# A software pipeline of attention and feed-forward: where the layer statistics and the transposed tokens stand in two engines' orders

## What is computed

```python
def _layer(x, wqkv, qs, ksc, wo, lg, lb, w1, b1, w2, b2):   # 8 heads of 64, window 64
    h = shift_token(x)                      # features 64..127 come from the token before
    q, k, v = split(h @ wqkv, 3)
    q = l2norm(q) * qs;  k = l2norm(k) * ksc
    q, k = rotary_xpos(q, k)
    x = x + local_attention(q, k, v) @ wo   # each window of 64 sees itself and the one before
    h = shift_token(x)
    mu = h.mean(-1, keepdims=True);  var = h.var(-1, keepdims=True)
    h = (h - mu) / jnp.sqrt(var + 1e-05) * lg + lb
    a, g = split(h @ w1 + b1, 2)            # 341 columns each
    return x + (a * gelu(g)) @ w2 + b2
```

## Time and profile before

| What | Value |
|---|---|
| median of 3 runs | 2008.37 us (2007.29 to 2013.43) |
| the profiled execution's own time | 2013.04 us |
| its span, first to last instruction | 2011.2 us |
| busy share of the span | PE 83%, DVE 65%, ACT 59%, POOL 54% |
| mean granted TensorE clock | 0.934 of full speed |

### The profile page before, as it was taken

How to read it: one execution, slowest core, us unless ns; L and a number is a source line. 1 busy time by engine, 2 the same in 40 slices (tenths; PEclk the granted TensorE clock), 3 DMA queues, 4 the chain that set the end, 5 groups by cost and what they waited for, 6 DMA issues and landing times. The chain is left out here.

```text
span 2011.2 us, 47115 instructions
## 1 busy us (share of the span) xinstructions
PE 1662.8 (83%) x18545; PEld 1149.5 (57%) x18545; DVE 1314.9 (65%) x2041; ACT 1195.2 (59%) x1972; POOL 1085.8 (54%) x631
## 2 busy tenths in 40 slices
PE   1389997899999348999999649899999899999953
PEld 1356665566666216776767426666666666666642
DVE  3378885555445508999999557777776766667532
ACT  0166666344444115777777428777787777777742
POOL 0166663344444206767677567666666666666403
PEclk9999999999999668999999879999999999999986
DMA  3100000000000020000000101111111111111101
GB/s 100 47 2 2 3 2 9 13 7 7 12 6 0 9 85 2 2 2 2 3 2 2 59 22 28 25 26 23 23 23 23 28 23 23 22 25 23 26 16 42
DMA packets 52352, 40.20 MB, mean 20 GB/s; under 512 B 24424, under 2 KB 44172, under 8 KB 52020
## 3 DMA queue, kind: packets, MB, share of 16 engines
q1 hardware_dynamic: 52148, 37.35, 7.3%
HBM read 15.75 MB, written 2.13 MB: 9 GB/s over the span
## 5 line engine op out<-in xcount | busy, mean ns | idle before, releaser
L438 POOL TENSOR_TENSOR a_prob<-a_prob,a_top 128x1024 f32<-128x1024 f32 x192 | 359.7, 1894 | 133.8 <-DVE a_top L651 133.8
L645 DVE TENSOR_TENSOR a_prob<-ps,a_table 128x1024 f32<-128x1024 f32 x192 | 226.2, 1220 | 112.9 <-PE ps L505 56.6
L612 ACT ACTIVATE a_probT<-ps 128x1024 f32<-128x1024 f32 x192 | 196.4, 1023 | 91.6 <-PE ps L515 91.6
L877 POOL TENSOR_TENSOR e_hh<-e_h,e_hh 128x512 fp32r<-128x512 f32 x112 | 144.2, 1290 | 197.1 <-ACT e_hh L864 195.4
L651 DVE TENSOR_REDUCE a_top<-a_prob 128x4 f32<-128x1024 f32 (+1 forms) x192 | 225.2, 1215 | 9.1 <-issue 0.4
L515 PEld LDWEIGHTS ps<-ident,a_prob 128*128 128x128 f32 x1536 | 168.7, 142 | 95.3 <-issue 61.0
L607 ACT ACTIVATE a_prob<-a_prob 128x1024 f32<-128x1024 f32 x192 | 202.4, 1054 | 32.5 <-POOL a_prob L438 32.5
L515 PE MATMUL ps<-ident,a_prob 128*128 128x128 f32 x1536 | 209.8, 280 | 7.6 <-ACT a_probT L612 2.6
L1115 POOL TENSOR_TENSOR i_qk<-i_raw,i_rot 128x1024 f32<-128x1024 f32 x64 | 151.9, 2374 | 83.6 <-ACT i_raw L1323 83.6
L1167 PE MATMUL ps<-i_wqkv,i_hT 128*128 128x512 f32 x256 | 144.6, 693 | 51.8 <-issue 25.1
L898 DVE TENSOR_TENSOR e_h<-ps,e_sg 128x512 f32<-128x512 f32 x112 | 77.4, 691 | 145.3 <-PE ps L764 124.7
(11 more groups left out here) (198 smaller groups left out, 3687.0 us busy)
## 6 DMA issues: line engine op xcount, KB each, us to landing
i_V<-i_V SPq DMA_DIRECT2D x96, 130.0 KB, 2.3
a_prob<-skew_scratch SPq DMA_DIRECT2D x2, 2048.0 KB, 9.4
X<-in_L_attn_x SPq DMA_DIRECT2D x4, 512.0 KB, 6.0
a_table<-in_c_l_table SPq DMA_DIRECT2D x1, 2048.0 KB, 8.2
e_xs<-Y SPq DMA_DIRECT2D x8, 256.0 KB, 2.3
i_ms<-Y SPq DMA_DIRECT2D x16, 128.0 KB
out_dram<-X SPq DMA_DIRECT2D x4, 512.0 KB, 3.3
i_ms<-Y SPq DMA_DIRECT2D x16, 127.0 KB
```

The costliest lines, as they stand in the source:

```text
L438: nc.gpsimd.tensor_tensor(s, s, top[:, slot].unsqueeze(2).broadcast_to([P, HG, KW]), ALU.subtract).then_inc(shifted, 1)
L612: nc.scalar.activation(probT[:, n % 4].rearrange("p (b n) -> p b n", b=2), ps[:, 4:6, :], ACT.Copy).then_inc(pT_sb, 1)
L645: nc.vector.tensor_tensor(prob[:, slot].rearrange("p (b x) k -> p b x k", b=2), ps[:, 2 * (n % 2):2 * (n % 2) + 2, :].rearrange("p b (x k) ...
```

## The change

Nothing is computed in another way but for one operation, which changes its engine. In each engine's loop over `step`:

- SP: `stage(R)` now comes ahead of `window_values(step + 1)` in its step.
- ScalarE: `inverse_deviation(R)` goes from the end of step 4R+6 into step 4R+7, behind `keep_probT` and ahead of `exp`. `keep_mlp_tokens(R)` is gone from ScalarE.
- VectorE: `deviations(R)` goes from the start of step 4R+7 to its end, behind `quotient`, and `keep_mlp_tokens(R)`, now a multiplication and an addition on VectorE, follows it at once. At the end of a step `keep_value` now stands ahead of `moments`.

```diff
@@ SP
             for step in range(FIRST, LAST):
-                if is_tile(step + 1):
-                    window_values(step + 1)
                 R, c = round_at(step, 5)
                 if R is not None and c == 0:
                     stage(R)
+                if is_tile(step + 1):
+                    window_values(step + 1)
@@ ScalarE
-            def keep_mlp_tokens(R):
-                l = layer(4 * R)
-                act.wait_ge(m_T, R + 1)
-                after(act, ga_ps, R * NC)
-                nc.scalar.activation(mT[:, :], ps[:, 0, :], ACT.Identity, scale=vecs[:, l, 0:1], bias=vecs[:, l, 1:2]).then_inc(m_sb, 1)
-
...
                 if is_tile(step - 1):
                     keep_probT(step - 1)
+                R, c = round_at(step, 7)
+                if R is not None and c == 0:
+                    inverse_deviation(R)
                 if is_tile(step):
                     exp(step)
...
-                R, c = round_at(step, 6)
-                if R is not None and c == 0:
-                    inverse_deviation(R)
-                R, c = round_at(step, 7)
-                if R is not None and c == 0:
-                    keep_mlp_tokens(R)
@@ VectorE
+            def keep_mlp_tokens(R):
+                l = layer(4 * R)
+                dve.wait_ge(m_T, R + 1)
+                after(dve, ga_ps, R * NC)
+                nc.vector.tensor_scalar(mT[:, :], ps[:, 0, :], vecs[:, l, 0:1], vecs[:, l, 1:2], ALU.mult, ALU.add).then_inc(m_sb, 1)
+
...
-                R, c = round_at(step, 7)
-                if R is not None and c == 0:
-                    deviations(R)
                 if is_tile(step + LEAD - 1):
                     square_sums(step + LEAD - 1)
...
                 if is_tile(step - 1):
                     quotient(step - 1)
+                R, c = round_at(step, 7)
+                if R is not None and c == 0:
+                    deviations(R)
+                    keep_mlp_tokens(R)
+                R, c = round_at(step, 8)
+                if R is not None and c < NC:
+                    keep_value(R, c)
                 R, c = round_at(step, 6)
                 if R is not None and c == 0:
                     moments(R)
-                R, c = round_at(step, 8)
-                if R is not None and c < NC:
-                    keep_value(R, c)
                 dve.drain()
```

## The result

| | Before | After |
|---|---|---|
| median | 2009.17 us (2007.29 to 2013.43) | 2023.5 us (2021.86 to 2024.25) |
| ratio, 95% interval | 1 | 1.0061 (1.0041 to 1.0082) |
| the profiled execution | 2013.04 us | 2024.25 us |

The changed kernel is slower by 14 us by the medians (by 12 by the ratio), where +6.8 was forecast: 2023.5 us against 2015. That is inside the range of 1992 to 2025, but above what rival A, the forecast, gave itself (2008 to 2022). To see where the time lies, both profiles are cut at three events: the first mask addition, the L1167 behind round 0's token copy, and the same L1167 twelve rounds later.

The account below looks back on a forecast made before the run. The bound was TensorE's 2.08 us wait for ScalarE's token copy each round, with the low clock behind it. Twelve rounds at +16.2 us and the ends at -9.4 gave +6.8, a median of 2015 us; range 1992 to 2025.

Parts of the forecast that it names:

- rival A: The forecast itself: deviations held beside GpSimd in step 4R+7, 2015 us, its own range 2008 to 2022; chance 0.47.
- Points 1 and 2: VectorE, end of step 4R+6: reduction starts 1.1 us earlier; ScalarE, start of step 4R+7: its work moves up 0.66 us.
- Point 3: VectorE, end of step 4R+7: a small deviation operation is held until GpSimd's L1118 ends, deviations end at 1702.35, not 1700.2.
- Point 4: TensorE's seam into step 4R+8: with the token copy on VectorE (0.75 us), L1167 starts 1.4 us later each round.
- Point 5: TensorE's clock: idle 4.1 us instead of 2.08, low stretch costs 1.4 us a round; twelve rounds make +16.2 us.
- rival D: Deviations held, with a second low-clock stretch in each round: 2.2 us a round for the clock, 2025 us; chance 0.10.
- C: Deviations held, but the low clock falls mostly on idle time: 0.7 us a round, 2007 us, no change; chance 0.18.
- Point 6: Sync queue: V copies' delay behind the stage stays hidden, some 8 us to spare; no wait and no gain in full rounds.
- Point 7: The ends gain: -4 us in round 0, 0 in round 13, -1.7 in round 14, -3.7 in round 15; sum -9.4.
- B: Deviations in step 4R+7 not held by GpSimd: L1167 starts 0.6 us earlier each round, 1992 us; chance 0.20.
- E: Nothing comes of the moves, because TensorE's dense work sets the round: 2008 us; chance 0.05.

Follow-up runs that it names:

- e9: The changed kernel with one wait more: GpSimd starts L1118 in step 4R+7 only when the deviations are done; 1986.4 us, ratio 0.9880.
- e1: The changed kernel with the deviations' refinement in nine small instructions, meant to read one SBUF tensor each, instead of three; 2036.3 us, ratio 1.0117.
- e5b: The changed kernel without the three operations that refine the deviations; 2003.0 us, ratio 0.9942.
- e3: The kernel before with seven unread 128x128 products filling TensorE's wait ahead of L1167 in step 4R+8; 1993.1 us, ratio 0.9900.
- e7b: The kernel before with the stage ahead of the V copies and seven unread products ahead of L1167 in step 4R+8; 1986.2 us, ratio 0.9858.
- e2: The changed kernel with fourteen unread 128x128 products filling TensorE's wait ahead of L1243; 1996.6 us, ratio 0.9914.
- e4: The kernel before with only the sync queue's part of the change, the stage ahead of the V copies; 1997.0 us, ratio 0.9915.
- e12: The changed kernel with the sync queue's old order, the V copies ahead of the stage; 2025.1 us, ratio 1.0081.
- e6b: The changed kernel with the deviations' refinement as twelve one-column operations; 2018.7 us, ratio 1.0027.

## Why the prediction was right, and what it sized wrong

Points 1 and 2 (moments, ScalarE's start of the step): as forecast. L1371's wait all but disappears, L1237 follows L1367 (0.65 us wait), and L1473 ends as L1181 does (1658.77).

Point 3 (the hold): right in kind, place and operation. The second small operation is caught, which is near what was taken (1702.35, with 1702.4 for the second); it ends 0.02 us behind L1118. L1243 waits 4.03 us against 4.1 forecast. e9 shows that GpSimd is the cause. What the text gave as the reason for these operations, two SBUF tensors read, is too narrow (e1, e5b). The forecast didn't hang on that.

Point 4 (the seam): the copy takes 0.81 (0.75 taken). With the clock out of play the seam costs 1.33 us in a steady round by e3 and 1.42 by e7b (1.4 forecast). Over twelve rounds it is 16.8 us by e7b, as forecast (twelve times 1.4), and 11.7 by e3 (564.3 - 552.6). The difference is the sync queue's: e3 has the old order, and its rounds after the first take 46.19 us in the mean, e7b's 45.83. (The forecast's own terms add up to 1704.2 for L1197's end, not 1704.1; nothing hangs on it.)

**Point 5 (the clock) is the term that was mis-sized.** It had 1.45 us a round before and 1.4 after, so no difference. The runs show 1.06 before (e3) and 2.23 after (e2): +1.17 a round, +14.1 over twelve. With the seam's 11.7 this is the +25.8 of the middle. With the new queue order on both sides (e4 and e7b for before) the parts are 16.8 for the seam, 11.6 for the clock and -2.6 for the order; either way the clock's share is what the forecast lacks. The error had two parts. The 1.45 came from a single undisturbed round (45.89) held against the mean of eleven (47.34); with the clock repaired the same eleven take 46.19, so 0.3 of the 1.45 was not the clock's. And the low stretch was priced as if it fell on the same work as before, where it only took L1167 (3.39 instead of 1.95). After the change the idle time lies ahead of L1243, the low stretch begins with L1243 and takes L1197 too, which alone loses 0.9 us, and in every second round it goes on and takes L1167 whole. Set against e2's durations, the first of the two rounds shown loses 0.16 + 0.89 + 0.50 = 1.6 us at L1243, L1197 and L1167, the second 0.42 + 0.89 + 1.56 = 2.9, in the mean 2.2. That is rival D's price, though the second stretch comes only in half of the rounds, and D's +26 for the middle is what was measured (+25.8).

So what A, C and D have in common, the hold, was right; where they part, at the clock, A failed and D was nearest. The time lies inside the range only because the range reached up to D's 2025, a case that was given a chance of 0.10; to that extent it was luck.

Point 6 (the sync queue): hidden for V, as forecast. That the stage in front "gains nothing in the full rounds" holds for the changed kernel (e12). In the kernel before the order alone was worth 0.85% (e4). There the moments stand ahead of `keep_value`, so a late stage can hold up the step; most of the gain that the profiles place is at the ends (6.8 of 9.4 us), and over the twelve rounds it is 2.6 us, 5.1 with the clock out of play (552.6 - 547.5), where the forecast has nothing. Gains of such edits need not add up: `keep_value` ahead of the moments and the stage ahead of V both remove the moments' wait for the stage.

Point 7 (the ends): -2.6 in round 0 (-4 forecast), -6.4 behind round 12 (-5.4), -9.0 together (-9.4). In round 0 L1243 still waits 2.58 us and L1197 behind it takes 1.93, where the forecast had the hold mostly over. At the end L1260 follows L1243 at 1975.78 without a wait for its gate, as forecast; TensorE's timeline of the changed kernel:

```profile
1974.90 1.09 PE L1243 MATMUL ps<-ident,i_mn 128*128 128x128 f32 x4 [11.27 <-DVE i_mn L1518]
1975.78 1.49 PE L1260 MATMUL ps<-i_w,i_A 128*128 128x128 f32 x6
```

Rivals B and E fell with L1243's wait of 4.03 us and with the +25.8 us of the twelve rounds. C, the low clock mostly on idle time, fell too: in every second round the clock falls 0.7 to 1.5 us before L1243 starts, but these are the rounds in which it stays low through L1167. Left open is why the length of the low stretch alternates from round to round; no run varied the distance between two waits alone.

## What to carry to other kernels

Small VectorE operations from SBUF to SBUF belong where GpSimd is idle. If they can't be put there and TensorE waits for them, let GpSimd wait for them, where its own result can come later: here one wait of 2.05 us on GpSimd took the kernel from 2023.5 to 1986.4 us.

A wait on TensorE is to be priced with the low clock behind it, on the instructions that stand there: here 4 us of idle time cost another 2.2. A few products that nobody reads, in a wait that can't be removed, gave 1.5% back in one kernel (ratio 1.0061 to 0.9914) and 1.0% in the other. And a change of several moves is worth taking apart: the stage ahead of V alone gained 0.85%, and the rest of the change lost more than that.

## What the runs showed of the hardware

- A VectorE operation need not read two SBUF tensors to be caught by GpSimd. `tensor_scalar` from SBUF to SBUF is caught with 4 columns and constants (1.66 us in e1, 0.17 at least) and with 128 columns and two operands per partition (2.39 at most in e5b, 0.34 in the median). The Trainium skill, page "SBUF — State Buffer", section "Who interferes with whom", names `tensor_scalar` among the operations that can take the ports shared with GpSimd, where it runs in a two-port mode; the trace agrees that it can be caught. The same operation with one column and an operand per partition was not stretched: 0.58 us for four of them beside a working GpSimd (e6b).
- Being caught has little to do with the size: an operation of 0.16 us lasts until GpSimd's instruction ends, up to 2.35 us (e2). When GpSimd waits instead and restarts, the next such operation is caught: in e9 the first 128x32 operation behind the token copy takes 0.92 us, not 0.19.
- Fourteen 128x128 products in f32 (3.29 us) in a 4 us wait keep the granted clock at 1.00 behind it. Seven are enough where the wait is 2 us: behind them L1167 takes 1.95 or 1.96 us in each of the rounds 1 to 12 (e3, e7b).
